# Attention features by split float32r products, the values (v) computed during routing, and expert rows 2p and 2p+1 side by side in one partition

## The reference

```python
qkv = x @ w_qkv                                    # x is xn here
z = einsum('bhtd,hdf->bhtf', q or k, proj)         # 16 heads of 8, 32 features each
prime = exp(z - max(z, axis=-1))
kv = einsum('bhtf,bhtd->bhfd', k_prime, v);  k_sum = sum(k_prime, axis=2)
out = einsum('bhtf,bhfd->bhtd', q_prime, kv) / (einsum('bhtf,bhf->bht', q_prime, k_sum) + 1e-6)
attention = out @ w_out + b_out

scores = (xn @ router_w.T + router_b) / max(temperature, 0.1)
gates = sinkhorn(scores, 3 iterations)             # row and column logsumexp, then exp, then / (sum + 1e-8)
top 2 of 8 experts, their gates divided by their sum + 1e-8
expert(t) = (relu(xn @ wg) * (xn @ wp)) @ wo       # 128 -> 256 -> 128
ffn = xn + sum over the two chosen experts of gate * expert(xn)
```

## Time and profile before

| | us |
|---|---|
| median of 3 runs (331.07 to 334.24) | 333.81 |
| the profiled execution, whole time | 333.39 |
| the profiled execution, span of the trace | 331.3 |
| PE busy in the span | 289.8 (87%) |
| DVE busy | 249.8 (75%) |
| POOL busy | 203.3 (61%) |
| ACT busy | 141.8 (43%) |
| scatter to slots_x (L449), median from issue to landing | 2.3 |
| load of a tile's rows (L328), median from issue to landing | 3.3 |

### The profile page before, as it was taken

How to read it: one execution, slowest core, us unless ns; L and a number is a source line. 1 busy time by engine, 2 the same in 40 slices (tenths; PEclk the granted TensorE clock), 3 DMA queues, 4 the chain that set the end, 5 groups by cost and what they waited for, 6 DMA issues and landing times.

```text
span 331.3 us, 6734 instructions
## 1 busy us (share of the span) xinstructions
PE 289.8 (87%) x1988; PEld 248.3 (75%) x1988; DVE 249.8 (75%) x619; ACT 141.8 (43%) x297; POOL 203.3 (61%) x303
## 2 busy tenths in 40 slices
PE   4996858899999999999996999999999999999300
PEld 4894336677777777887776999999999999779200
DVE  4866788856787777777775899999999997772283
ACT  3494432033444455554543555555555554452000
POOL 4000000188888788888500388888888888888391
PEclk9999585659999999999996999999999999999755
DMA  7974000011211111219220488888878871111793
GB/s 239 349 259 147 1 2 16 1 53 61 71 60 69 51 69 60 69 61 309 81 67 0 118 250 237 250 244 258 253 240 248 253 208 49 40 48 49 221 406 134
DMA packets 33749, 46.43 MB, mean 140 GB/s; under 512 B 5472, under 2 KB 22368, under 8 KB 33728
## 3 DMA queue, kind: packets, MB, share of 16 engines
q1 hardware_dynamic: 28608, 36.19, 35.6%
q0 software_dynamic: 4544, 9.84, 8.4%
q10 hardware_dynamic: 576, 0.15, 0.2%
HBM read 27.17 MB, written 17.68 MB: 135 GB/s over the span
## 4 chain that ended last, share of the span: by engine, by line
PE 70%; DVE 10%; POOL 7%; DMA 5%; issue 3%; ACT 1%; SPq 1%; DVEq 0%; POOLq 0%
PE bank L533 14%; PE bank L704 10%; PE bank L554 6%; PE bank L578 6%; PE bank L692 5%; PE bank L693 5%; PE bank L694 5%; POOL rows_y L457 4%; PE bank L568 3%; PE bank L487 3%; DMA x_tile<-slots_x 3%; PE bank L677 3%; PE bank L504 2%; PE bank L540 2%; DVE acc L987 2%
## 5 line engine op out<-in xcount | busy, mean ns | idle before, releaser
L449 POOL DMA_INDIRECT slots_x<-xn,slot_i x64 | 63.3, 989 | 70.8 <-DVE slot_i L1088 60.0
L457 POOL DMA_INDIRECT rows_y<-xn,row_i x78 | 80.6, 1034 | 38.6 <-DVE xn L1175 25.4
L776 ACT ACTIVATE feat<-z_sb 128x512 f32<-128x512 f32 x64 | 39.9, 631 | 72.2 <-DVE z_sb L943 72.1
L936 DVE TENSOR_REDUCE neg_max<-bank 128x16 f32<-128x512 f32 x64 | 43.8, 686 | 28.4 <-PE bank L533 28.4
L692 PE MATMUL bank<-xT_high,w_high 128*128 128x256 f32 x156 | 48.2, 309 | 1.2 <-DVE w_low L1183 1.2
L693 PE MATMUL bank<-xT_low,w_high 128*128 128x256 f32 x156 | 45.0, 288 | 0.0
L694 PE MATMUL bank<-xT_high,w_low 128*128 128x256 f32 x156 | 44.7, 286 | 0.0
L943 DVE TENSOR_TENSOR z_sb<-bank,neg_max 128x512 f32<-128x512 f32 x64 | 42.5, 682 | 1.4
L704 PE MATMUL bank<-w_tile,hidden 128*128 128x128 f32 x312 | 41.3, 275 | 0.0
L533 PE MATMUL bank<-w_feat,xT_stage 128*128 128x512 f32 x80 | 40.1, 603 | 0.0
L704 PEld LDWEIGHTS bank<-w_tile,hidden 128*128 128x128 f32 x312 | 38.2, 192 | 0.1
(11 more groups left out here) (140 smaller groups left out, 489.2 us busy)
## 6 DMA issues: line engine op xcount, KB each, us to landing
w_tile<-w_expert_dram SPq DMA_DIRECT2D x39, 384.0 KB, 3.7
slots_x<-zeros SPq DMA_DIRECT2D x39, 144.0 KB, 2.3
x_tile<-slots_x SPq DMA_DIRECT2D x39, 130.0 KB, 3.3
acc<-x_dram SPq DMA_DIRECT2D x8, 256.0 KB, 5.5
xn<-rows_y SPq DMA_DIRECT2D x8, 256.0 KB, 5.6
w_tile<-rows_y SPq DMA_DIRECT2D x8, 256.0 KB, 5.8
out_dram<-acc SPq DMA_DIRECT2D x8, 256.0 KB, 3.4
xT_stage<-xnT SPq DMA_DIRECT2D x10, 128.0 KB, 2.0
```

The source lines that it names most:

```text
L449: pool.indirect_dma_start(slots_x, bass.IndirectOffsetOnAxis(slot_i[k][:, i:i + 1], 0), xn[:, j, :], None).then_inc(scattered[n % FLIGHT], 16)
L457: pool.indirect_dma_start(rows_y, bass.IndirectOffsetOnAxis(row_i[:, k, t:t + 1], 0), y_tile(k, t), None)\
L776: act.activation(feat[par][n][:, :], z_sb[n][:, :], ACT.Exp).then_inc(feat_ready, 1)
L936: dve.tensor_reduce(neg_max[n][:, :], args(n), AX_X, ALU.max, negate=True).then_inc(z_negmax, 1)
```

## The change

- **z**: each 128x512 float32 product becomes three float32r products of 128x512 (`xnT_high`, `xnT_low`, `w_feat_high`, `w_feat_low`). DVE splits the feature weights in the prologue; POOL splits xnT, a cast and a subtraction for each of 8 groups, after it has done DVE's half of the normalisation.
- **v**: all 8 groups of values are computed by PE in the routing links, copied by ACT, and lie in `v_aug` for all tiles. `xT_stage` and its DMAs are gone, and the loop is written out.
- **Routing**: the bias is scaled ahead, the gates' sums are taken by POOL beside `choose`, which works on unnormalised gates; the two count products are float32r; `place` has fewer steps and counts in slots instead of tiles.
- **Prologue**: the feature weights come first, PE starts after 8 instead of 24 idle products, with two more ahead of each group.
- **Early batches**: 14 instead of 13, POOL held to 5 scatters a batch. The first two experts' weights are split ahead of the last early batch. PE has 10 idle products around the first expert rows.
- **Expert rows**: rows 2p and 2p+1 of a tile go to partition p, so one partition's load is one run of 1152 bytes instead of two runs of 520. After each tile POOL clears one column of `gap`.
- **End**: two late batches. POOL adds both planes of groups 0 to 3 straight to acc, DVE those of groups 4 to 7; SP and ACT each store half. DVE's last attention steps stand between its sums.

```diff
...
-    EARLY = 13
+    EARLY = 14
     FLIGHT = 4
-    PER_BATCH = 6
-    LEAD = 6
+    PER_TWO = 10
...
-            for b in range(1, LOOP_FROM):
-                step(b, b // 2, b % 2)
-            with engine.Fori(LOOP_FROM // 2, EARLY // 2) as i:
-                step(2 * i, i, 0)
-                step(2 * i + 1, i, 1)
-            for b in range(EARLY // 2 * 2, EARLY):
+            for b in range(1, EARLY):
+                if b == EARLY - 1 and ahead_of_last:
+                    ahead_of_last()
                 step(b, b // 2, b % 2)
...
+        def combine(engine, k, g, added, before):
+
+            engine.wait_ge(plane_landed[k][g], 16)
+            if k == 1:
+                engine.wait_ge(added, TOPK * before + 1)
+            tiles = acc[:, g * GROUP:(g + 1) * GROUP, :].rearrange("p j d -> p (j d)")
+            engine.tensor_tensor(tiles, y_plane(k, g), tiles, ALU.add).then_inc(added, 1)
 
...
-            def stage(f_half, par):
-
-
-                f = 2 * f_half + par
-                sp.wait_ge(z_ready, 4 * (f - 1))
-                sp.wait_ge(v_ready, f - 1)
-                cols = bass.ds(f * (2 * P), 2 * P)
-                sp.dma_start(xT_stage[par][:, :], xnT[:, cols]).then_inc(xT_staged[par], 16)
-
...
-            xs = slots_x.rearrange("(k t p) d -> k p t d", t=2, p=P)
+            xs = slots_x.rearrange("(k p t) d -> k p (t d)", t=2, p=P)
 
             def load_rows(k, q, r):
                 if late(k, LOOP):
                     sp.wait_ge(y_copied, k - LOOP + 1)
-                sp.dma_start(x_tile[r][:, :, :],
-                             xs[bass.ds(k, 1), :, :, 0:USED].rearrange("a p t d -> (a p) t d"))\
+                sp.dma_start(x_tile[r][:, :, :].rearrange("p t d -> p (t d)"),
+                             xs[bass.ds(k, 1), :, :].rearrange("a p n -> (a p) n"))\
                     .then_inc(rows_landed[r], 16)
...
+            for n in range(NG // 2):
+                for g in (n, NG // 2 + n):
+                    for k in range(TOPK):
+                        sp.dma_start(y_plane(k, g), planes[k, :, g * GROUP * D:(g + 1) * GROUP * D])\
+                            .then_inc(plane_landed[k][g], 16)
+
+            for g in range(NG // 2):
+                store_group(sp, g, added_by_pool, g)
             sp.wait_ge(out_stored, 16 * NG)
...
+            for g in range(NG):
+                pool.wait_ge(rstd_done, g + 1)
+                for t in range(GROUP - BY_ACT):
+                    j = g * GROUP + t
+                    ins = pool.tensor_scalar(xn[:, j, 0:D], acc[:, j, :], moments[:, j, 0:1], rstd[:, j:j + 1],
+                                             ALU.subtract, ALU.mult)
+                ins.then_inc(xn_by_pool, 1)
+
+            for g in range(NG):
+                cols = slice(g * GROUP * P, (g + 1) * GROUP * P)
+                pool.wait_ge(xnT_copied, g + 1)
+                pool.tensor_copy(by_token_tile(xnT_high[:, cols]), xnT_group(g)).then_inc(xnT_rounded, 1)
+                pool.wait_ge(xnT_rounded, g + 1)
+                pool.tensor_tensor(by_token_tile(xnT_low[:, cols]), xnT_group(g), by_token_tile(xnT_high[:, cols].bitcast(F32)),
+                                   ALU.subtract)\
+                    .then_inc(xnT_split, 1)
+
+            def set_ones(g):
+                pool.wait_ge(v_ready, g + 1)
+                pool.wait_ge(xnT_split, g + 1)
+                pool.memset(v_group(g)[:, :, VC:AUG], 1.0).then_inc(ones_set, 1)
 
             def half_tile(n):
 
...
-                    pool.wait_ge(z_shifted, 4 * LOOP_FROM - LEAD + 4 * n // PER_BATCH)
+                    pool.wait_ge(z_shifted, 4 * LOOP_FROM - LEAD + 8 * n // PER_TWO)
...
+                pool.memset(gap[:, k:k + 1], 0.0)
 
             pool.wait_ge(acc_added, EARLY - 1)
             for k in range(SLOT_TILES):
                 send_rows(k)
 
...
+            pool.wait_ge(bias_added, 2 * NT)
+            pool.wait_ge(acc_added, GROUP // 2 * (NG // 2))
+            for n in range(NG // 2):
+                for k in range(TOPK):
+                    combine(pool, k, n, added_by_pool, n)
...
-            pe.wait_ge(consts_set, CONSTS)
-            keep_warm(24, 4)
+            pe.wait_ge(consts_set, 2)
+            keep_warm(8, 4)
+            pe.wait_ge(feature_weights_landed, 16 * N_FEATURE_WEIGHTS)
+            feature_weights()
             pe.wait_ge(ident_set, 1)
-            pe.wait_ge(feature_weights_landed, 16 * N_FEATURE_WEIGHTS)
             for g in range(NG):
+                keep_warm(2, 4)
                 transposes(g)
                 if g >= 1:
                     router(g - 1)
-                    keep_warm(1, 4)
...
+            def z(n, f):
+
+                if n == 0:
+                    pe.wait_ge(xnT_split, f // 2 + 1)
                 if late(f, 1):
                     pe.wait_ge(z_shifted, 4 * f + n - 3)
-                pe.matmul(bank[Z_BANK + n][:, :], xT(f, par, n % 2), w_feat[:, n // 2, :],
-                          start=True, stop=True).then_inc(z_ready, 1)
-
-            def v(f, par):
-                if late(f, 1):
-                    pe.wait_ge(v_copied, f)
-                for h in range(2):
-                    mm = pe.matmul(bank[V_BANK][:, h * P:(h + 1) * P], xT(f, par, h),
-                                   wv_sb[:, :], start=True, stop=True)
+                to, half, qk = bank[Z_BANK + n][:, :], n % 2, n // 2
+                pe.matmul(to, xT(xnT_high, f, half), w_feat_high[:, qk, :], start=True, stop=False)
+                pe.matmul(to, xT(xnT_high, f, half), w_feat_low[:, qk, :], start=False, stop=False)
+                pe.matmul(to, xT(xnT_low, f, half), w_feat_high[:, qk, :], start=False, stop=True).then_inc(z_ready, 1)
+
...
+                        pe.matmul(bank[ROUTE_BANK][:, 0:W], earlier_r[:, :], mask[:, :], start=True, stop=True)
+                        pe.matmul(bank[ROUTE_BANK][:, W:2 * W], ones_r[:, :], mask[:, :], start=True, stop=True)\
                             .then_inc(counts_ready, 1)
                 elif part == 2:
...
+                    values(2 * (n // 5))
                     pe.wait_ge(row_normed, n // 5 + 1)
...
+            keep_warm(6, 4)
             rows_T(0, 0, 0)
             rows_T(1, 0, 1)
+            keep_warm(4, 4)
             up(0, 0, 0)
+            pe.wait_ge(att_ready, EARLY)
...
-                for t in range(GROUP - BY_ACT):
-                    j = g * GROUP + t
-                    ins = dve.tensor_scalar(xn[:, j, 0:D], acc[:, j, :], moments[:, j, 0:1], rstd[:, j:j + 1],
-                                            ALU.subtract, ALU.mult)
-                ins.then_inc(xn_by_dve, 1)
-
+
+            dve.wait_ge(proj_landed, 16)
+            dve.wait_ge(head_set, 3)
+            dve.tensor_tensor(proj_diag[:, :, :], over_tiles(proj_sb, HEADS), wide(head_of_row, F), ALU.mult)\
+                .then_inc(diag_ready, 1)
             for g in range(NG + 1):
                 if g < NG:
                     statistics(g)
                 if g >= 1:
-                    normalise(g - 1)
-                if g == 1:
...
-                    settle(dve.tensor_reduce(gate_sum[:, :], by_tile(gate_exp), AX_X, ALU.add))
-                    settle(dve.tensor_scalar(gate_sum[:, :], gate_sum[:, :], GATE_EPS, None, ALU.add))
-                    settle(dve.reciprocal(gate_inv[:, :], gate_sum[:, :]))
-                    settle(dve.tensor_tensor(by_tile(gates), by_tile(gate_exp), wide(gate_inv, E), ALU.mult))
-                    choose(0, gates)
...
-                settle(dve.tensor_copy(totals[:, :, :].rearrange("p e i -> p i e"),
-                                       bank[ROUTE_BANK][:, W:2 * W].rearrange("p (i e) -> p i e", e=E)))
...
+            attend_early(dve, step, first_weights_low)
+            denominators(EARLY - 1)
+            invert(EARLY - 1)
+            divide(EARLY - 1)
...
+            for b in range(EARLY, NB):
+                step(b, b // 2, b % 2, front=b + 1 < NB)
+            dve.wait_ge(bias_added, 2 * NT)
+            combine_group(0)
+            denominators(NB - 1)
+            invert(NB - 1)
+            divide(NB - 1)
+            combine_group(1)
+            combine_group(2)
+            add_projection(NB - 1)
+            combine_group(3)
...
```

320 lines of the change are left out of this document (170 added, 150 removed).

## The result

The changed kernel takes 323.54 us, median of 6 runs (321.89 to 324.39), and the kernel before 333.6 us in 6 runs on the same chip (331.07 to 334.24). The ratio is 0.9692, 95% interval 0.9651 to 0.9733: 10.1 us or 3.1% less. The forecast was 316.5 us, range 308 to 325. The direction is right and the time is in the range, but 7 us of the expected 17 are missing, and it lies nearest to the 322 and 325 us of two rivals that did not come about. The profiled execution took 323.77 us with a span of 321.8, which the forecast's sum puts at 314.5.

A forecast was written before the change was run, and what follows sets the result against it. The prediction took the moment of POOL's first expert row, hanging on PE's early batches, then POOL's scatters, as the bound: 333.4 - 5.2 - 3.2 - 7.5 - 3.2 + 2.3 = 316.6, forecast 316.5 us, range 308 to 325.

The forecast's parts named there:

- The bound and the path: Whole kernel: time is prologue, routing, early batches, start of the experts, POOL's 117.85 us between scatters of results, and 26.6.
- Prologue, -5.2: Up to the last router products: end at 23.0 instead of 28.2 us, with PE's transposes starting at 8.9, 1.76 a group.
- Routing, 32.0 us: From the last router products to slot_i: 32.0 instead of 35.2 us, -3.2, so slot_i at 55.0.
- Early batches, 101.2 us: First kv of batch 1 to last early numden: 13 batches at 7.75 us, 101.2 in all, end 7.5 earlier at 159.6.
- rival 5: Early batches: a 512-column float32r product costs more than twice 0.11, at 0.45 giving 352 us; chance 0.03.
- rival 1: Early batches: DVE takes over from PE, 8.4 us a batch instead of 7.75, giving 325 us; chance 0.12.
- 1.8 for a start at low clock: Early batches: 1.8 us added to the thirteen batches' sum because they start at low clock.
- Start of the experts, 8.1 us: Last early numden to POOL's first scatter of results: 8.1 instead of 11.3 us, by weights split already and idle products.
- POOL's phase, +2.3 for gap: First to last scatter of results: clearing gap costs 0.06 us a tile, 2.3 us more.
- The rows as one piece: POOL's expert phase: loading expert rows as one piece of 1152 bytes gains 0, as PE's waits lie under POOL's shadow.
- End, 0: From POOL's last scatter to the end: no change, sixteen sums as before, both engines slowing each other; bounds -3 and +3.
- rival 2: Experts' start: rows come late, as scatters at 1.6 us end 6 us later and PE waits, 322 us; chance 0.08.

The follow-up runs named there:

- x6_no_gap: The changed kernel without the one-column memset of gap that POOL does after each tile's two scatters of results; 320.34 us, ratio 0.9616 to the kernel before.
- x3_early13: The changed kernel with 13 early batches instead of 14 and twelve scatters allowed in two batches instead of ten; 317.11 us, ratio 0.9545 to the kernel before.
- c3_plus_bias: c1_13_late_nogap with x9_warm_long's dummy products, and 28 of 64 bias pieces added in POOL's idle time before its first scatter of results; 306.62 us.
- x4_warm: The changed kernel with thirteen small dummy products in PE's idle stretches between 48 and 60 us, six of them ahead of batch 1's kv; 322.28 us.
- x2_v_back: The changed kernel with two dummy products, the size of v's, put back into every batch outside routing; 330.84 us, ratio 0.9949 to the kernel before.
- x1_z2: The changed kernel with z made of two of its three products (low activations times high feature weights left out); 319.17 us, ratio 0.9613 to the kernel before.
- x9_warm_long: x4_warm with 21 dummy products instead of 6 ahead of batch 1's kv; median 320.59 us, four runs from 317.3 to 323.64.
- x7_split_late: The changed kernel with the first two experts' weights split behind the early batches again, not ahead of the last one; 321.38 us.
- c1_13_late_nogap: The changed kernel with the edits of x3_early13, x7_split_late and x6_no_gap together; 314.96 us, ratio 0.9499 to the kernel before.
- x8_rows_apart: The changed kernel with rows p and p + 128 in partition p again, loaded as two pieces of 130 numbers; 323.01 us, ratio 0.968 to the kernel before.
- x5_feat_after_g1: The changed kernel with the feature-weight products moved back behind the transposes of group 1; 327.68 us, ratio 0.9844 to the kernel before.

## Why the prediction was right, and where it was not

- **The bound and the path: right.** POOL's scatters of results set the second half, and the moment of the first one counts. x6_no_gap, x3_early13 and c3_plus_bias each moved POOL's start or pace, and the time followed.
- **Prologue, -5.2: too large.** Measured -1.9 in the profile (26.3 instead of 28.2). The group step was right (1.78 against 1.76); the start was wrong, since the wait for the router's weights and products at twice their time put PE 2.8 us behind 8.9. In x4_warm the products followed each other in 1.0 us and the router's end was at 24.0.
- **Routing, 32.0 us: measured 30.2.** The conflicts with POOL were sized at 2 us for four passes. They cost 0.1 to 0.2 in the changed kernel's profile and 1.5 in x4_warm's. By the Trainium skill's rule ("SBUF — State Buffer", Who interferes with whom), that two such instructions exclude each other for a whole one, each could lose up to POOL's 1.27, an estimate. The trace agrees: the largest loss was 1.1 (1.51 against 0.42 with POOL idle), where 1.23 us of POOL's instruction were left, and every pass ended 0.27 to 0.29 us after POOL's instruction. What the forecast had no hold on is when the two meet, and in the changed kernel they met near the end of POOL's instructions: the cost was near nothing by luck of the phase. Prologue and routing together missed by 1.5 us, slot_i at 56.5 against 55.0.
- **Early batches, 101.2 us: measured 106.9. This is the step that failed.** The pitch was right to 0.1 us, 1.3 in sum, and so were its terms: 0.45 for v (x2_v_back) and 0.23 for a 512-column product. That rules out rival 5, and rival 1 too: PE leads (x1_z2). What was mis-sized is the edges. "1.8 for a start at low clock" measured 3.7 (x9_warm_long). And the split ahead of the last batch was entered as a gain of the experts' start alone; it puts 2.2 us on the batch before the last, as DVE holds `att` behind it (x7_split_late). For this moved step I had not counted what it is put ahead of. Pitch, start and split make 1.3 + 1.9 + 2.2 = 5.4 of the 5.7.
- **Start of the experts, 8.1 us: measured 8.3.** The size is right and one of its two reasons wrong: with the weights split late it is 8.4. What is left to shorten it from 11.3 is the other one, the idle products and with them the granted clock, 1.00 from 166.55 to 174.86, where it was 0.52. In c1_13_late_nogap, where it was 0.83 from 155.31 to 165.19, the way from the first transposes to POOL's first row took 8.9 us (160.41 to 169.31), and 7.1 in the changed kernel (167.80 to 174.86). No run changed the clock there alone.
- **POOL's phase, +2.3 for gap: measured +3.2,** within the bounds (0 to 5), and 3.4 without it (x6_no_gap). The rows as one piece: 0, as said (x8_rows_apart).
- **End, 0: measured -0.7.** Two queues for the stores and another order of the sums moved it little; the sums of both engines still slow each other (a sum of DVE takes 1.61 beside POOL, 0.69 alone). No run took these parts one by one.

Against the forecast of the span: 321.8 - 314.5 = 7.3 = 3.3 - 1.8 - 0.2 (first kv 3.2 instead of 3.4 after slot_i) + 5.7 + 0.2 + 0.9 - 0.7, to the rounding. The number fell into the range by its width, not by a rival foreseen: the upper part was drawn for a late row (rival 2) and a slower batch (rival 1), and what filled it were the two edges, which no rival named.

What stays open: what makes the feature-weight products take 0.9 us each in some executions and 1.8 in others. x5_feat_after_g1's expectation says half clock for the slow ones of the changed kernel; the recorded clock does not bear that out. It reads 1.00 from 7 to 12 us in both the changed kernel and x4_warm, and 0.50 at 9 to 11 in c1_13_late_nogap.
